# Degree embeddings of a graph network: row gathers in the node stage replaced by one-hot products inside an earlier sum

## The reference, cut to what matters

```python
in_deg  = minimum(segment_sum(ones, dst), 511)
out_deg = minimum(segment_sum(ones, src), 511)
sum3d   = segment_sum(edge_attr @ W_sum + b_sum, src)
gnn     = xn + z_in[in_deg] + z_out[out_deg] + sigmoid(cent * W_cent + b_cent) \
             + sigmoid(vor * W_vor + b_vor) + sum3d
mix     = linear attention over the nodes (q, k, v; k and v normed per head; k^T v / n) @ w_out + b_out
x       = x + gnn + mix                # xn = layernorm(x)
x       = x + moe_ffn(layernorm(x))    # 8 experts, top 2
```

## Time and profile before

| | us |
|---|---|
| median of 3 runs (2528.39 to 2532.34) | 2530.14 |
| the profiled execution | 2524.97 |
| its span, first to last instruction | 2522.7 |
| edge stage, first to last row add on POOL | 24.0 to 1623.2 |
| node stage, to the last of its rows | 1623 to 1817 |
| routing | 1817 to 1900 |
| FFN | 1900 to 2522.7 |

### The profile page before, as it was taken

How to read it: one execution, slowest core, us unless ns; L and a number is a source line. 1 busy time by engine, 2 the same in 40 slices (tenths; PEclk the granted TensorE clock), 3 DMA queues, 4 the chain that set the end, 5 groups by cost and what they waited for, 6 DMA issues and landing times.

```text
span 2522.7 us, 33934 instructions
## 1 busy us (share of the span) xinstructions
PE 1669.0 (66%) x10955; PEld 1289.7 (51%) x10955; DVE 1246.7 (49%) x3232; ACT 725.7 (29%) x1605; POOL 1690.2 (67%) x1107
## 2 busy tenths in 40 slices
PE   2444345455666666666566765277668999999997
PEld 1211123333443444444455554266567888888886
DVE  2343333343444444444355654245695666666664
ACT  1011113233333322333121111044443444444442
POOL 2767767677888888888888888888504444444442
PEclk7556657777788787878788786599889999999999
DMA  9998887886655555555555554589735888888885
GB/s 287 206 145 142 130 136 126 120 131 97 91 67 73 66 74 71 69 70 71 73 68 73 66 73 50 80 157 180 168 126 177 260 261 256 262 256 246 256 262 163
DMA packets 417548, 358.56 MB, mean 142 GB/s; under 512 B 43353, under 2 KB 341050, under 8 KB 417372
## 3 DMA queue, kind: packets, MB, share of 16 engines
q1 hardware_dynamic: 270492, 264.31, 35.8%
q0 software_dynamic: 146880, 92.09, 33.8%
HBM read 247.03 MB, written 109.25 MB: 141 GB/s over the span
## 4 chain that ended last, share of the span: by engine, by line
DMA 45%; POOL 20%; PE 20%; issue 10%; DVE 2%; SPq 2%; POOLq 0%; ACT 0%; ACTq 0%; DVEq 0%
DMA node_table<-edge_sums,row_i 32%; POOL node_table L1424 20%; PE bank L669 9%; PE bank L683 8%; DMA state<-L_gnn_z_in,in_deg 6%; DMA big<-w_parts 5%; PE bank L638 1%; PE bank L640 1%; PE bank L655 1%; SPq L1494 1%; DMA peak_rows<-peaks 0%; DMA node_numbers<-id_rows 0%; DMA b2r<-L_ffn_b 0%; POOLq L1424 0%; DMA big<-b_peak_rows 0%
## 5 line engine op out<-in xcount | busy, mean ns | idle before, releaser
L1424 POOL DMA_INDIRECT node_table<-edge_sums,row_i x782 | 1250.1, 1599 | 367.2 <-DMA node_table<-edge_sums,row_i 178.1
L452 PE MATMUL bank<-edge_rows,same_node 128*128 128x130 f32 x1564 | 316.7, 354 | 583.7 <-issue 372.3
L452 PEld LDWEIGHTS bank<-edge_rows,same_node 128*128 128x128 f32 x1564 | 269.3, 251 | 734.2 <-issue 690.9
L1235 ACT COPY edge_sums<-bank 128x390 f32<-128x390 f32 (+1 forms) x261 | 126.4, 484 | 1207.4 <-DMA node_table<-edge_sums,row_i 1146.8
L1469 POOL DMA_INDIRECT result<-mixw,slot_tok x105 | 167.5, 1595 | 304.8 <-DVE mixw L1191 159.6
L1378 ACT ACTIVATE mixw<-bank,m_r 128x256 f32<-128x256 f32 (+1 forms) x456 | 242.0, 549 | 351.1 <-PE bank L669 226.7
L669 PE MATMUL bank<-edge_rows,big 128*128 128x256 f16 (+1 forms) x2736 | 289.7, 266 | 24.4 <-DMA big<-w_parts 23.3
L683 PE MATMUL bank<-big 128*128 128x256 f16 x2520 | 284.4, 273 | 1.0 <-issue 1.0
L669 PEld LDWEIGHTS bank<-edge_rows,big 128*128 128x128 f16 x2736 | 250.8, 99 | 58.2 <-DMA big<-w_parts 28.9
L769 DVE SCALAR_TENSOR_TENSOR dup<-edge_sums,thresh,to_spare 128x6 f32<-128x6 f32 x131 | 29.3, 224 | 464.4 <-ACT edge_sums L1235 464.4
L683 PEld LDWEIGHTS bank<-big 128*128 128x128 f16 x2520 | 244.2, 98 | 28.5 <-issue 1.3
(11 more groups left out here) (256 smaller groups left out, 2344.1 us busy)
## 6 DMA issues: line engine op xcount, KB each, us to landing
big<-w_parts SPq DMA_DIRECT2D x114, 1024.0 KB, 8.8
edge_rows<-edge_attr SPq DMA_DIRECT2D x130, 384.0 KB, 3.9
big<-L_ffn_W SPq DMA_DIRECT2D x128, 128.0 KB, 3.6
w_parts<-big SPq DMA_DIRECT2D x64, 256.0 KB, 4.2
node_table<-zeros SPq DMA_DIRECT2D x20, 645.0 KB, 8.3
node_table<-edge_sums,row_i POOLq DMA_INDIRECT x782, 3.6
mixw<-node_table SPq DMA_DIRECT2D x96, 129.0 KB, 3.8
b2r<-L_ffn_b SPq DMA_DIRECT2D x57, 128.0 KB, 8.1
```

Of the source, the lines that this page charges most:

```text
L452: ins = e.matmul(ps_sum[:, i * XW:(i + 1) * XW], S[:, g % SRING, i * P:(i + 1) * P], X[:, c // LOAD % XRING, c % LOAD, :], start=True, sto ...
L1235: e.copy(O[:, g % ORING, 0:n, :], ps_sum[:, 0:n * XW].rearrange("p (a b) -> p a b", a=n)).then_inc(edge_kept, 1)
L1424: e.indirect_dma_start(table[t], bass.IndirectOffsetOnAxis(ap=row_i[:, g % ORING, i:i + 1], axis=0), O[:, g % ORING, i, 0:RW], None, compu ...
```

## The change

- The out-degree is counted as the in-degree is, by one-hots of src. A degree step now handles one of the two counts of a group (dst in even steps, src in odd ones), so there are 522 counting steps and a last one that clips and turns the counts. They run at 3.6 a tick from tick 10 (to about tick 156). Each count has one buffer of one-hots where there were two for the one count.
- The counts are stored to HBM as f16 rows and loaded back broadcast to all partitions, four node tiles at a time; eight comparisons with `lane_k` per four tiles give one-hots of the degrees (`deg_hot_z`).
- z_in and z_out are loaded once and split into three bf16 parts each (10 VectorE operations on 128x1024). In the rest, 24 bf16 products of 128x256 per tile (2 tables, 4 chunks of 128 degrees, 3 parts) add both rows in `ps_rest`.
- b_out and count times b_sum are one product with `bias_m`, with a ScalarE copy per tile.
- The gathers, the column of ones, the reductions over it and the product with b_sum leave the node stage. A table's row is 512 B.
- The side steps are 270: mix from step 60, a tile every 2 steps instead of 3, to 165; the rest from 168, a tile every 2 steps instead of 1. Node stage: 49 + 13 ticks, PE takes the tables' rows 3 ticks after SP's step instead of 4.
- The shared buffer of the edge rows holds later small tensors, so that the new ones fit.

```diff
-XW = EDIM + 2
-RW = EDIM + 1
+XW = EDIM + 1
+RW = EDIM
...
-DEGREES = 1.5
+DEGREES = 3.6
+DEG_AT = START + 2
...
-MIX0, MIX_EVERY = NORM_END + 16, 3
-FOLD0 = MIX0 + (TILES - 1) * MIX_EVERY + 11
-REST0 = FOLD0 + 3
-SIDE_STEPS = REST0 + TILES + 3
+Z0 = NORM_END + 2
+MIX0, MIX_EVERY = NORM_END + 31, 2
+FOLD0 = MIX0 + (TILES - 1) * MIX_EVERY + 9
+REST0, REST_EVERY = FOLD0 + 3, 2
...
     def tensor_degree(e, d):
-        b = d - 1
+        b, i = divmod(d - 2, 2)
         if 0 <= b < GROUPS:
-            e.wait_ge(deg_hot, b + 1)
+            e.wait_ge(deg_hot, 2 * b + i + 1)
...
     def tensor_rest(e, u):
...
             for k in range(KC):
                 e.matmul(ps_rest[t % 4][:, 0:DIM], xnT[:, t, k, :], mq[:, k, :], start=(k == 0), stop=False)
-            e.matmul(ps_rest[t % 4][:, 0:DIM], ones, b_out0, start=False, stop=False)
+            e.wait_ge(bias_made, t + 1)
+            e.matmul(ps_rest[t % 4][:, 0:DIM], bias_s[:, t % 2, :], bias_m, start=False, stop=False)
+            e.wait_ge(z_hot, t // ZT + 1)
+            for i in range(2):
+                for k in range(ZK):
+                    for a in range(3):
+                        ins = e.matmul(ps_rest[t % 4][:, 0:DIM], deg_hot_z[:, t // ZT % 2, i, k, t % ZT, :], zp[:, i, a, k, :],
+                                       start=False, stop=False)
+            ins.then_inc(z_added, 1)
...
+    def vector_degree(e, d):
+        b, i = divmod(d, 2)
+        if b < GROUPS:
+            lo, n = b * GROUP, len(tiles_of(b))
+            hi_of, lo_of = ((dst_hi, dst_lo), (src_h, src_l))[i]
+            if d == 0:
+                e.wait_ge(idx_dve, IDX_DST)
+            if b:
+                e.wait_ge(deg_summed, 2 * (b - 1) + i + 1)
+            e.tensor_tensor(hotA[:, i, 0:n * TILES].rearrange("p (a b) -> p a b", a=n),
+                            iotab[:, 0:TILES].unsqueeze(1).to_broadcast([P, n, TILES]),
+                            hi_of[:, lo:lo + n].unsqueeze(2).to_broadcast([P, n, TILES]), ALU.is_equal)
+            e.tensor_tensor(hotB[:, i, 0:n * P].rearrange("p (a b) -> p a b", a=n),
+                            iotab.unsqueeze(1).to_broadcast([P, n, P]),
+                            lo_of[:, lo:lo + n].unsqueeze(2).to_broadcast([P, n, P]), ALU.is_equal).then_inc(deg_hot, 1)
...
-    def pool_nodes(e, tick):
-        t = tick - 4
-        if 0 <= t < TILES:
-            e.wait_ge(n_degree, 2 * t + 2)
-            e.wait_ge(zin_added[t % 4], 16 * (t // 4 + 1))
-            if t >= 4:
-                e.wait_ge(zout_added[t % 4], 16 * (t // 4))
-            e.indirect_dma_start(state[:, t, :], None, z_out, bass.IndirectOffsetOnAxis(ap=out_deg[:, t:t + 1], axis=0),
-                                 compute_op=ALU.add, bounds_check=DEG - 1, oob_is_err=True).then_inc(zout_added[t % 4], 16)
...
-            e.indirect_dma_start(state[:, t, :], None, z_in, bass.IndirectOffsetOnAxis(ap=in_deg[:, t:t + 1], axis=0),
-                                 compute_op=ALU.add, bounds_check=DEG - 1, oob_is_err=True).then_inc(zin_added[t % 4], 16)
```

More of the change, by code:

```diff
@@ L38 @@
 assert 2 * P <= 3 * PAD
-ZERO = 645
+ZERO = 640
 PIECES = 5
@@ L697, in tensor_program @@
                 tensor_rest(e, u)
-        for tick in range(TILES + 14):
+        for tick in range(TILES + 13):
             tensor_nodes(e, tick)
@@ new lines, in vector_z @@
+    def vector_z(e, u):
+        i, s = divmod(u - Z0, 5)
+        if not 0 <= i < 2:
+            return
+        v = z_raw[i]
+        if i == 0 and s == 0:
+            for t in range(TABLES):
+                e.wait_ge(table_zero[t], 16 * PIECES)
+            e.wait_ge(pad_zero, 96)
+        if s == 0:
+            e.wait_ge(z_load, 16 * (i + 1))
+        elif s:
+            e.wait_ge(z_split, 5 * i + s)
+        if s % 2 == 0:
+            e.tensor_copy(zp[:, i, s // 2], v).then_inc(z_split, 1)
+        else:
+            e.tensor_tensor(v, v, zp[:, i, s // 2], ALU.subtract).then_inc(z_split, 1)
@@ L1475, in pool_program @@
             pool_edges(e, tick)
-        for tick in range(TILES + 4):
-            pool_nodes(e, tick)
         for j in range(XG - 1):
@@ L1715, in sync_program @@
                 sync_mix(e, u)
-        for tick in range(TILES + 14):
+                sync_rest(e, u)
+        for tick in range(TILES + 13):
             sync_nodes(e, tick)
```

268 lines of the change are left out of this document (155 added, 113 removed).

## The result

The kernel after takes 2434.8 us (median, 2432.2 to 2435.2), the kernel before beside it 2529.5: a ratio of 0.962, 95% interval [0.9605, 0.9638]. Forecast were 2497 us and 2440 to 2560. Two later comparisons on other chips gave 0.966 [0.964, 0.969] and 0.964 [0.960, 0.967].

What follows compares the result with a forecast made beforehand. POOL was taken to bound the edge stage from 660 us and the node stage. Terms -60 - 15 + 24 + 25 - 8 + 1 = -33 us took 2525.0 to 2492; with 5.2 for the median, 2497 us, range 2440 to 2560.

Steps and rivals of the forecast that it cites:

- PE in the mix, +24: Edge stage, ticks 92 to 156: PE becomes the bound, 6.05 us a tick against 5.67, +24 us (ends +5, +72).
- The 0.08 us stalls are hidden here, since POOL is not the bound: Mix, ticks 92 to 156: holds of row adds by degree steps, 0.08 us each, cost nothing beside PE.
- 91 + 33 us: PE's added work in 60 ticks from 660 us: 12.5 more mix tiles, 91 us, and 126 more degree steps, 33 us.
- A fuller PE should get more of it, worth up to a tenth: Mix: a busier PE is granted more clock than 0.81, worth up to a tenth.
- Node stage, -60: Node stage without gathers: 2.4 us a tile instead of 3.72, -60 us (ends -74, -35).
- The fill at the front gives nothing: Start of the node stage: set by the table's first loads, so no gain there.
- Ticks 10 to 92, +25: First part of the edge stage: 295 new degree steps, +12 stalls and +13 late rows, +25 us (ends 0, +60).
- Rows of 512 B, -8: Shorter table rows make row adds cheaper where POOL waits for DMAs, -8 us (ends 0, -40).
- End of the edge stage, -15: Counting done by tick 156: the starved call's 6.9 us and late stalls go, lane_k comparisons come; -15 us (ends -20, +15).
- The rest, 0: Ticks 162 to 256: 24 new products a tile on PE hidden under POOL's 5.57 us a tick, 0; +40 at low clock.
- The fourth: Rival, edge stage: extra work fits in gaps and shorter rows shorten waits, 2441 us; chance 0.14.
- The first: Rival, edge stage: runs of hot steps hold POOL's row adds to the run's end, 98 + 70 us, 2653 us; chance 0.14.

Runs made afterwards that it cites:

- a_kv_twice: Kernel after with each k and v product of the mix made twice; 2530.5 us, 1.002 of the kernel before.
- a_rows_516: Kernel after with table rows of 129 floats (516 B) again instead of 128 (512 B); 0.969 of the kernel before.
- b_no_gathers: Kernel before with both gathers of z left out of the node stage, the product with b_sum kept; 0.974 of the kernel before.
- b_degrees_even: Kernel before with 1.65 degree steps a tick instead of 1.5, so none is left for the last tick; 0.9985 of the kernel before.
- a_no_z: Kernel after without the 24 one-hot products a tile and the lane_k comparisons, z added nowhere; 0.9645 of the kernel before.
- a_degrees_7: Kernel after with 7.2 degree steps a tick instead of 3.6, in runs of seven; 1.001 of the kernel before.

## Why the prediction was wrong

The gain was 95 us where 33 were forecast; the spans of the first two traces differ by 90, 57 more than forecast. By the table, the node stage with its start has 26 us of these 57, the mix 21, the first part 14 and the end of the edge stage 4, while the part behind the node stage was 8 slower.

- **PE in the mix, +24, measured +3 to +5, and none of that is PE. This is the step that failed.** The forecast had PE as the bound of ticks 92 to 156, at 5.8 us of work and 6.05 with waits against POOL's 5.57. In fact PE did 255 us of work in 340, 4.3 us a tick and 5.3 with its waits for `hotB`; POOL waited for `row_i` for 1.5 us, its idle time was 54.9 us before and after, and the +3 to +5 are holds. "The 0.08 us stalls are hidden here, since POOL is not the bound" is wrong with it. That PE can become the bound there is true (a_kv_twice), but at twice the k and v products. The terms were wrong: 91 + 33 us are sums of groups, added to PE's busy time, in which groups overlap (they sum to 262 us where 225 are busy in the kernel before, and to 296 where 255 are in the kernel after); and each was priced at clock 0.81, while 1.6 times the mix work brought 0.91 to 0.93. "A fuller PE should get more of it, worth up to a tenth" was written down and not put into the sum.
- **Node stage, -60, measured -85.** The mechanism was right (gathers gone, PE next), the size was not, and it is the largest part of the miss. PE was put at 2.1 us a tile from a stretch at clock 0.94, DMA at 2.2, and 2.4 was taken above both. At full clock PE runs a tile in 1.87 us without a gap, and DMA never bound, at 0.61 busy and 182 GB/s. "The fill at the front gives nothing" missed 4 us.
- **Ticks 10 to 92, +25, measured +18 to +19.** Near in size, but not for its reasons: it was +12 for holds, half of 24 being hidden, and +13 for rows that come late. On the chip of a_rows_516 all else is equal, 516 B rows too: row adds 1 to 271 took 632.9 us against 613.7 and 614.9 in b_no_gathers and b_degrees_even, which are the kernel before up to there. Holds are 16 us of that, idle time 3. So the holds were the smaller number of the two (0.06 us a step and not 0.08), none of them were hidden, and late rows cost next to nothing: POOL waited 0.3 us for `row_i` in a_rows_516, and 0.6 to 3.3 us in the kernels with 512 B rows and 3.6 steps a tick, but for a_kv_twice.
- **Rows of 512 B, -8,** measured -13 and -23 on the first 271 adds and -10 and -13 in the medians: within its ends. Between the kernels before and after POOL's idle time fell by less, 14 and 4 us in the two pairs of traces, where the single change gave 17 and 19.5; 3 us of that are the new work's, the rest is open.
- **End of the edge stage, -15, measured -18.** Right, though a_no_z shows the comparisons with `lane_k` at nothing and b_degrees_even the 8.47 us call at less than its 6.9.
- **The rest, 0:** right, with more room than was claimed.
- **Rivals.** The fourth, an edge stage that takes it all for nothing, 2441 us, was nearest; it was given 0.14. The first is a true mechanism, but at runs of three or four steps it costs 17 to 18 us up to row add 271 and 4 to 6 in the mix, where the rival had 98 and 70; with runs of seven it is 105 us more again. The earlier trace rows could have told that a hold need not last to the end of a run: its call was let go after one operation. The mean row add forecast up to 1000 us was 1.60 to 1.68 (1.653 came up to 660, 1.605 from there to 1000), 1.56 behind (1.558), the clock over 0.9 in the mix (0.93), and PE did wait for `hotB` there (60.9 us); POOL's waits for `row_i`, the last row add at 1650 (1610) and the node stage at 135 us (110) were wrong.

The range failed as its lower end of 2440 joined a good edge stage with the forecast's node stage; no case held both better.

## What to carry to other kernels

When work is added to an engine that now idles, price it also at the clock of a stretch where it is full, and do not add sums of overlapping groups to busy time; then give both ends. Split a stage of the bounding engine into its idle time and the excess of its calls: the two told here what no total did. Count an engine's own waits into its margin: PE was the bound at 84% busy. Keep runs of two-input SBUF operations on VectorE short while POOL issues indirect DMAs: over the first 270 row adds the holds were 9 or 10 us with no early steps, 22 with 1.8 steps a tick, 26 to 32 with 3.6 (34 and 36 in two kernels with more work on PE), and 137 with 7.2.

## What was not expected of the hardware

- A row add caught by a run of VectorE operations with two SBUF inputs mostly ended 1.42 us after the run's end, up to 6.89 us in all in a_degrees_7 and 8.47 in the kernel before, while another begun inside such a run took 1.60.
- The same fp32 product of 512 columns took 791, 662 and 610 ns at granted clocks of 0.81, 0.93 and 0.98.
- 4 B more in a row of 512 B made its packet 5 ns dearer (82 to 87) and cost 13 and 23 us over 270 row adds in two pairs of traces, 10 and 13 us in their medians, where DMA was 0.80 to 0.84 busy.
